# One program part for a whole patch-embedding, state-space and mixture-of-experts layer, with the late blocks behind the last routed unit

## The reference

```python
h = tok(x)                     # 64 images -> 196 patches: real 2-D FFT of 16x16x3 pixels, weights,
                               # projection to D=192, class token, positions: (64, 197, 192)
h = h + ssm(layernorm(h))      # y = causal convolution over the 197 tokens, one kernel K[d] for each channel,
                               # K = einsum(C * B_bar, exp(delta*A*l)) from 64 complex states
n = layernorm(h)
probs = softmax(n @ router_w); gates, idx = top_k(probs, 2); gates = gates / sum(gates)
routed = sum_e dense_g[e] * ((silu(n @ w_gate[e]) * (n @ w_up[e])) @ w_down[e])     # 8 experts, width 192
shared = (silu(n @ ws_gate) * (n @ ws_up)) @ ws_down                                # width 768
alpha  = sigmoid(n @ sg_w + sg_b)
out = h + alpha * shared + (1 - alpha) * routed                                     # 12608 tokens
```

## Time and profile before

| | us |
|---|---|
| median of 3 executions | 1256.18 |
| lowest, highest | 1250.46, 1256.38 |
| the profiled execution, its time | 1252.63 |
| its span, first to last instruction | 1250.8 |
| busy in the span: PE, DVE, POOL, ACT | 1040.9, 868.9, 656.7, 537.4 |
| mean granted clock of TensorE | 0.946 |

### The profile page before, as it was taken

The page is one execution under the profiler, slowest core; times in us unless marked ns, Lnnn a source line. Parts: engine busy times, 40 slices in busy tenths (PEclk is TensorE's granted clock), DMA queues, the critical chain, the costliest instruction groups (busy, mean ns, idle before and its releaser), DMA issues. The chain is left out here.

```text
span 1250.8 us, 24364 instructions
## 1 busy us (share of the span) xinstructions
PE 1040.9 (83%) x7867; PEld 718.1 (57%) x7868; DVE 868.9 (69%) x2637; ACT 537.4 (43%) x1023; POOL 656.7 (53%) x682
## 2 busy tenths in 40 slices
PE   5977997684599998999999996888878878864997
PEld 5967886684365655656666663444444445432555
DVE  6999776322487788888788765566666666651998
ACT  1233533222455555555556541444444444431332
POOL 0134413000377776777777752376766776763543
PEclk9989999788699999999999998899999999996999
DMA  8678786866995435454333216565555555333997
GB/s 298 239 238 268 231 257 161 212 132 172 203 211 148 123 90 135 121 129 97 93 87 97 69 49 184 117 126 111 129 113 118 123 115 135 94 86 112 306 299 241
DMA packets 285967, 196.08 MB, mean 157 GB/s; under 512 B 178840, under 2 KB 264602, under 8 KB 285590
## 3 DMA queue, kind: packets, MB, share of 16 engines
q1 hardware_dynamic: 251152, 142.46, 44.6%
q0 software_dynamic: 19488, 39.17, 9.3%
q10 hardware_dynamic: 15206, 12.93, 4.0%
HBM read 100.52 MB, written 74.65 MB: 140 GB/s over the span
## 5 line engine op out<-in xcount | busy, mean ns | idle before, releaser
L1728 POOL DMA_INDIRECT parts<-unit_yu,unit_token x208 | 215.9, 1038 | 97.2 <-issue 47.4
L1310 POOL DMA_INDIRECT routed<-rows_w,slot x198 | 216.6, 1094 | 64.1 <-issue 64.1
L1492 DVE SCALAR_TENSOR_TENSOR hf<-psu,sg 128x512 f32<-128x512 f32 x120 | 82.8, 690 | 83.8 <-ACT sg L1233 40.3
L1160 PE MATMUL pso<-ffn_w_hi,hh 128*128 128x192 f16 x480 | 119.4, 249 | 23.0 <-DVE hl L1497 18.0
L1233 ACT ACTIVATE sg<-psg 128x512 f32<-128x512 f32 x120 | 71.8, 599 | 147.3 <-PE psg L1145 114.2
L454 POOL TENSOR_TENSOR e_rs<-e_ve,mhalf 98x8 f32<-98x8 f32 x16 | 49.8, 3114 | 138.3 <-DVE e_ve L692 131.4
L1160 PE MATMUL pso<-ffn_w_hi,hl 128*128 128x192 f16 x480 | 119.2, 248 | 0.3 <-issue 0.3
L1160 PE MATMUL pso<-ffn_w_lo,hh 128*128 128x192 f16 x480 | 119.1, 248 | 0.0
L1145 PE MATMUL psg<-xt,ffn_w_hi 128*128 128x512 f16 x360 | 118.9, 385 | 0.0
L1145 PE MATMUL psu<-xt,ffn_w_hi 128*128 128x512 f16 x360 | 118.0, 382 | 0.3 <-issue 0.3
L524 PE MATMUL ps<-w,area 128*98 128x192 f32 x528 | 99.9, 333 | 0.0
(11 more groups left out here) (245 smaller groups left out, 2817.9 us busy)
## 6 DMA issues: line engine op xcount, KB each, us to landing
end_part<-parts SPq DMA_DIRECT2D x48, 384.0 KB, 5.6
area<-in_xa_dram SPq DMA_DIRECT2D x33, 392.0 KB, 5.5
area<-in_xb_dram SPq DMA_DIRECT2D x33, 392.0 KB, 6.2
resid<-spare ACTq DMA_DIRECT2D x32, 294.0 KB
hin<-resid SPq DMA_DIRECT2D x24, 384.0 KB
yin<-mixed SPq DMA_DIRECT2D x96, 96.0 KB
spare<-in_xa_dram SPq DMA_DIRECT2D x15, 392.0 KB, 6.1
spare<-in_xb_dram SPq DMA_DIRECT2D x15, 392.0 KB, 7.6
```

The source lines that it names most:

```text
L1160: last = nc.tensor.matmul(o, hx[m % 2][:, ts], wd[k][:, m], start=(a == 0 and m == 0 and t % 2 == 0), stop=(a == 2 and m == NSH - 1), skip ...
L1310: nc.gpsimd.indirect_dma_start(out=routed[:, :], out_offset=bass.IndirectOffsetOnAxis(ap=slot[q][:, k, t:t + 1], axis=0), in_=rows_w[q][:, ...
L1492: nc.vector.scalar_tensor_tensor(out=hf[i][:], in0=psu[:, i], scalar=1.0 / SCALE, in1=sg[i][:], op0=ALU.mult, op1=ALU.mult).then_inc(s["hf ...
L1728: nc.gpsimd.indirect_dma_start(out=parts[:, :], out_offset=bass.IndirectOffsetOnAxis(ap=token[q][:, k:k + 1], axis=0), in_=y[q][:, k, :], ...
```

## The change

All five stages stand in one program part. Each stage's function now returns one function per engine, and `feed_forward` calls them in a row in a single `nc.Block()`. Where the meetings were, single semaphores stand: PE waits for `u_ready` and the two class-row transfers before the convolution, for `corners` (the cleared corners) at each first use of a tile, for `y0` and `y1` before the first transposes; ACT and DVE wait for the stored rows (`rows_stored`) before the first eviction, because the evictions overwrite them; SP waits for the `parts` to have landed (`r_sent0`, `r_sent1`) before it loads them; PE's first down product of the last stage waits for the last results of the units to have been read (`r_y_d`, `r_y_a`).

Three steps move. The class rows: DVE multiplies them before the eviction of group 2 and ACT stores them before group 3, instead of ahead of the convolution. The corners of the four `toeplitz` tiles are cleared behind the first product. In the last stage the first `combine` stands in chunk 6 instead of chunk 2, and from there one stands in every chunk, also in those with `token_out`. Some buffers are allocated in another order. `NLATE` stays at 5.

```diff
@@ feed_forward
-        shared_expert(nc, io, t, ...)
-        routed_experts(nc, t, weights, routed, parts)
-        finish(nc, t, weights, parts, out)
+        shared = shared_expert(nc, io, ctx, sems, t, ...)
+        experts = routed_experts(nc, ctx, sems, t, weights, routed, parts)
+        end = finish(nc, ctx, sems, t, weights, parts, out)
+        block = ctx.enter_context(nc.Block())
+        @block.tensor
+        def _(pe):
+            embedded["tensor"](pe)
+            mixing["tensor"](pe)
+            mixing["read"](pe)
+            shared["tensor"](pe)
+            n = experts["tensor"](pe)
+            end["tensor"](pe, n)
...
@@ mix
+                if n == HG + 3:
+                    sp.wait_ge(u_ready, NG + 1)
+                    sp.wait_ge(out_done, 16 * 2)
                 load(n)
...
+        def vector(dve):
+            embedded["rows_stored"](dve)
             for n in range(NCG):
+                if n == 2:
+                    embedded["class_products"](dve)
                 dve.wait_ge(conv1, n + 1)
+                if n == 0:
+                    for tile in t:
+                        clear_corners(nc, tile, corners)
...
@@ shared_expert, gpsimd
-            for q in range(NR):
-                tiles_sent = sum(tiles(b) for b in range(q, NBLK, NR))
-                pool.wait_ge(s[f"sent{q}"], 32 * tiles_sent)
@@ shared_expert, sync
             sp.wait_ge(s["fillers"], 16 * (NFILL + 1 + E))
+            sp.wait_ge(s["carried"], NBLK)
+            for q in range(NR):
+                sp.wait_ge(s[f"sent{q}"], 32 * sum(tiles(b) for b in range(q, NBLK, NR)))
...
@@ finish
+        def sync(sp, units):
             n = [0]
+            for q in range(2):
+                sp.wait_ge(sems[f"r_sent{q}"], 64 * units)
+            sp.wait_ge(sems["r_turn"], 64 * units)
...
+                if c == 0:
+                    pe.wait_ge(sems["r_y_d"], 2 * units)
+                    pe.wait_ge(sems["r_y_a"], 2 * units)
...
                 if c % NSH == 1 and c > NSH:
                     token_out(NOW + c // NSH - 1)
-                elif c >= 2:
+                while done < c + 1 - FIRST_COMBINED:
                     combine(done)
                     done += 1
```

More of the change, by code:

```diff
@@ L886, in load_constants, with feed_forward @@
     return k
-def feed_forward(nc, io, spare, area, block_stored, y_stored, weights, resid, mixed, routed, parts, out, consts):
+def feed_forward(nc, io, embedded, mixing, spare, area, block_stored, y_stored, weights, resid, mixed, routed, parts, out, consts):
     with ExitStack() as ctx:
@@ L924, in sums_of, with shared_expert @@
     return t["sums"][part][:, at:at + nt]
-def shared_expert(nc, io, t, spare, area, block_stored, y_stored, weights, resid, mixed, routed, out, consts):
+def shared_expert(nc, io, outer, sems, t, spare, area, block_stored, y_stored, weights, resid, mixed, routed, out, consts):
     with ExitStack() as ctx:
@@ L1742, in _, with vector @@
             send(2 * n - 1, 1)
[L1743 to L1748 removed]
+        def vector(dve):
+            n = pairs(nc.vector, dve)
             S = slice(128 - H1, 128)
@@ L1814, in finish @@
         xt, alpha = t["xt"], t["alpha"]
-        y = [sb(f"part{i}", [128, 2, NT, D]) for i in range(RING)]
+        y = [sb(f"part{i}", [128, 2, NT, D]) for i in range(RING - 1)]
+        sb("gap", [128, 40])
         sg = [weights["stage"][0][:, i * BT:(i + 1) * BT] for i in range(2)]
```

247 lines of the change are left out of this document (140 added, 107 removed).

## The result

The kernel after takes 1243.64 us in the median of 20 executions (1235.33 to 1249.68), the kernel before, beside it, 1253.87 us (1247.94 to 1262.5). The ratio is 0.9931, with a 95% interval from 0.9915 to 0.9947: about 9 us faster, where I had forecast 18. On two other chips the same two kernels were measured again: 0.9937 (0.9914 to 0.9960) and 0.9917 (0.9889 to 0.9945) on one, 0.9901 (0.9874 to 0.9927) on the other. So 8 to 12 us of the forecast 18 are there, by chip.

What follows compares the result with a forecast made beforehand. No engine is busy throughout, so it read TensorE's waits around the four meetings. Gains of 0 + 0 + 2.9 + 15.1 = 18.0 us off 1252.63 gave 1234, range 1227 to 1246.

Steps and rivals of the forecast that it cites:

- the four additions on DVE: Late blocks, chunks 6 to 29: four more combines at 1.2 us each, 4.8 us in all, bounds 0.87 and 2.07 each.
- the main term: Removing the meeting between units and late blocks: 15.1 us gained, 11.7 to 16.4 by the price of the additions.
- the second meeting: Between convolution (mix) and shared expert: 0 gained, bounds 0 and +0.5, since SP waited 2.9 us for `mixed` behind it.
- The first meeting: Between embedding and convolution: PE starts about 6 us earlier but waits at group 6; 0 gained, bounds -2 and +6.2.
- The third meeting: Between shared expert and units: unit loads and first unit products start 2.9 us earlier; bounds +2 and +4.
- The rival by which all 6 us arrive: Convolution follows its earlier start and all 6.2 us arrive: 1228; chance 0.09.
- the one by which the convolution stays at half clock: Convolution: PE, stopped at group 6, stays at half clock, up to 2.3 us lost per later group: 1262; chance 0.05.
- The fourth meeting: Between units and late blocks: PE goes on at 1129.9, SP's loads start near 1139; 15.1 us gained.
- The rival of scattered rows that land late: Late blocks: landing rows, not the part's end, held the loads, first sum ready at 1153.6 as before: 1238; chance 0.10.
- Their rival (1240): Late blocks: transfers set the pace, 29.5 MB at 296 GB/s taking 99.6 us from 1139: 1240; chance 0.20.

Runs made afterwards that it cites:

- skip_token: Kernel after with DVE's additions from chunk 5 on, none in the four chunks that have a token_out; 0.9892 of the kernel before.
- skip_cut2: Kernel after with additions from chunk 5, none in the four token_out chunks, and the second meeting put back; 0.9875 of the kernel before.
- the quiet one: Pair of unchanged kernel before and unchanged kernel after on one chip, units' stages of nearly one length; spans 1191.3 and 1177.2 us.
- small_add: Kernel after with POOL adding only 8 of each 192 columns, a probe and no candidate; 0.9898 of the kernel before.
- before_again: Kernel before, unchanged, run for a second trace on another chip; 1244.61 us.
- cut4_order: Kernel after with the last meeting put back and the kernel before's order of additions on DVE; 1.0013 of the kernel before.
- three: Kernel after with convolution loads reordered, first late products ahead of the last unit's down products, combine from chunk 5; 0.9924 of the kernel before.
- after_again: Kernel after, unchanged; 0.9937 of the kernel before. Its theory B: longer program part slows the units' loop, again 5 to 7 us longer.
- after_third: Kernel after, unchanged, as its job's common reference and third trace of the units' stage; 0.9917 of the kernel before.
- early_first: Kernel after with SP loading convolution groups 6 to 11 as soon as their tiles are free, toeplitz tiles between; 0.9907 of the kernel before.

## Why the prediction was wrong

Two steps failed: the price of the four additions on DVE, in the main term, and the 0 for the second meeting. The first meeting was off by 1 to 2 us. The rest of the mechanism came as forecast.

**The third meeting** was right in the traces: 2.9 forecast, 7.8 less 4.7 to 5.0 us measured.

**The first meeting**: forecast 0, with PE's start near 222.3 (222.35) and a wait of 6 us at group 6 (3.2 to 4.1 in the four traces of after). The convolution ends 1.2 us later than before on the average of four traces of after (297.3 against 296.1 in three of before), inside the 2 us that I had allowed. The mechanism holds, the size was off by 1. I had the six early groups end at 237.8; they ended at 240.1, because the granted clock was 0.50 up to 226 us and 0.62 from there to 230, and PE waited 0.55 us for an eviction of DVE, which had been clearing corners. Behind the wait the clock fell once more, as shown above. The rival by which all 6 us arrive is out, and so is the one by which the convolution stays at half clock.

**The second meeting**: this step failed. I had taken "SP waited 2.9 us for `mixed` behind the meeting" for a proof that its removal does nothing, with bounds of 0 and +0.5 gained. I had left out that the work around a meeting can also get slower without it. From the last product to the transposes it costs 2 us in the traces (the times of skip_token and skip_cut2, 1.1 us apart, are too close to part). A bound that excludes a loss needs a reason, and I had given none.

**The fourth meeting**: forecast 15.1 us, measured 13.1 in the first pair, 13.7 in the quiet one. The start was as forecast: the first `hidden` 2.5 us behind the last unit product (2.3 and 2.6 measured), chunk 6 16.9 behind that (18.2 and 16.6), SP's loads 1.3 to 2.1 us behind the last scatter. The rival of scattered rows that land late is out. What was mis-sized is the term of the four additions: I priced it at 4.8 us, with an upper bound of 8.3, and the stretch grew by 5.8 in the first pair and by 8.8 in the quiet one. The wrong step was the price of one, 0.87 us for the `combine` itself and at most 1.20 more for a `low` beside POOL, and of that "I take 1.2, near the lower end, since in two of the four chunks before there was some slack of PE's". The slack was there and was used up, 4.75 us in the stretch before and 0.2 after. But DVE's busy time rose by 10.3 us, 2.6 for each added `combine`, more than the bound of 2.07. In the new order the `combine`s fall beside POOL's additions, which before had met `low` and only one `combine`: the `combine`s of the whole stretch, and not only the four, are 1.57 us on the average and not 1.03 (36.1 us for 23, 19.6 for 19). That one stands in the trace of before, so the row from which to price it was there:

```profile
1189.95 2.57 DVE L1959 TENSOR_TENSOR spare<-spare,end_part 128x768 f32<-128x768 f32 x1
```

That skip_token took back 5.9 of the 8.8 leaves 3 us that hang on the rest of the new order or on POOL's loads, which now run ahead of the chunks.

**The transfers.** Their rival (1240) named a limit that lies near, but not by the rate that my text gave it. From the first load of `parts` to the end of the last store the kernel after takes 94.4 to 99.0 us, and with nearly no work on POOL 90.8, at 327 GB/s. I had taken 296 GB/s for the limit and got 99.6 us, which the chip then beat; the rate of before was no limit of the DMA engines. So 90.8 us bounds what the transfers need from above, 4 to 8 us under the kernel after. With skip_token the transfers show in the tail; for small_add's small gain they are argued and not shown.

**The sum** on a quiet chip: 3.0 (third meeting) + 13.7 (fourth) - 1.8 (convolution) - 2.1 (behind it) = 12.8 us, against a measured 11.9 in the medians (0.9901). With my 2.9, 15.1, 0 and 0 I was 5 too high: 1.4 in the main term, 2.1 in the second meeting, 1.8 in the first.

**What stays open** are 2 to 4 us more on the chips on which the kernel takes 1245 or 1254 us. On these, ACT stands still in the units with all its inputs ready, for up to 7 us, as in the row of 1129.41 above, where PE had finished `u_short` at 1122.4. The view names no engine of the program as the releaser and writes `remote`. DVE and POOL have such stops too. In the seven such traces without the last meeting the units' stage takes 342 to 358 us, in the three with it (before, before_again, cut4_order) 344 to 351. The means differ by 2 us, with `three` or without it, and the sets scatter by 16 and 7, so whether the kernel after is slower there or was only caught so, these traces can't tell. After_again came out as its theory B has it, with units 8 us longer than before_again's; after_third's are 3 us longer, and small_add's and early_first's, with the same code there, no longer. The stops themselves are no longer in the kernel after: ACT's add up to 124, 120 and 123 us in its three traces on these chips, each taken whole, and to 128 and 126 in the two of before. That it isn't the placement of buffers is shown only for a chip without the stops.

## What to carry to other kernels

A meeting of the engines costs what the next stage's last input could have gained, and no more: 6 us of earlier start gave nothing where the stage has its own pace, and 3 us gave 3 in the traces where a load stood first behind the meeting. The large price (13 us) was where one engine's end of part, behind its last scatters, held everybody. And when an engine gains time, ask what fills it: here the engine that was second, DVE, took 6 to 9 us of the gain back. An instruction that is moved has to be priced where it will stand: `combine` took 0.95 us where POOL was idle and up to 2.57 beside its additions.

## What the runs showed of the hardware

- Ending a program part behind indirect transfers of POOL costs 7 to 8 us. SP's next load comes 9.6 us behind the last scatter's issue with the meeting of the kernel before (four traces), 8.3 in the two in which the first four stages share a part, and 1.3 to 2.1 without it (fourteen). In the four the load lies 17.1 to 20.4 us behind PE's last product but always 9.6 behind the scatter, so it is POOL's end that the others wait for. Since the loads wait for the landed rows, the landing is over within 1.3 us of the last issue in ten of the fourteen.
- An addition of POOL (128x768, 1.8 us alone) makes one of DVE's steps on two SBUF inputs 1.2 to 1.6 us longer: `combine` takes 0.95 or 2.56 us, `low` 0.68 or up to 2.3. `hidden` and `token_out`, which take one input from PSUM, never take more than 0.69 and 0.42 us in any of the twenty traces. On the average an addition cost 1.1 us of DVE. The Trainium skill (SBUF — State Buffer, "Who interferes with whom") says that a VectorE instruction with two SBUF inputs and a GpSimd instruction that reads SBUF contend for a port pair that only one of them holds at a time. If every addition met such steps of DVE for its whole length and DVE always came second, the 36 us would have cost DVE 36 (an estimate from that rule), and they cost 25. The trace agrees in kind; DVE loses less, since part of POOL's time falls beside steps that read PSUM, and POOL is held up as well (its additions take up to 2.5 us).
- One kernel takes 1254, 1245 or 1196 us from chip to chip at the same granted clock (0.946, 0.949, 0.948). Of the 60 and 51 us between the spans, 50 and 43 are in the units, where the slower chips have stops of this kind (no releaser in the view; in the two rows shown the inputs were there): over a trace 36 to 48 of ACT, 20 to 30 of DVE and 21 to 26 of POOL. What causes them is open. One, in the trace of after_again:

```profile
1108.09 0.59 ACT L1767 ACTIVATE stage<-u_short 64x512 f32<-64x512 f32 x1 [7.36 <-remote]
```

  On the chips of 1196 us no such stop, of any engine, is in any of ten traces. A gain measured on one chip is not the gain on another.
